# Sixteen squared sums and 48 PSUM copies moved from VectorE to ScalarE in a list-scheduled eight-core attention and feed-forward kernel

## What is computed

```python
z      = gelu_tanh(ln(x))
zn     = z / max(norm(z), 1e-12)                # per token
sim    = zn @ zn.T                              # per batch, 4096 x 4096
seq    = max of sim over earlier tokens         # strictly causal
ema    = zn . ema_norm                          # used alone for token 0
gate   = 1 - a + a * exp(-tau * (w * seq + (1 - w) * ema))
x      = x + z * gate
y      = ln(x)
g      = softmax(y @ gate_w.T)                  # 8 experts
x      = x + y @ weight.T + (1/16) * sum_e g_e * (y @ U_e.T) @ V_e.T
```

## Time and profile before

| | us |
|---|---|
| median of 2 runs | 374.4 (374.09 to 374.71) |
| the profiled execution, its own time | 373.94 |
| span of the slowest core in it (core 0) | 372.3 |
| span of the shortest core in it (core 6) | 362.0 |
| mean granted TensorE clock, core 0 / core 6 | 0.953 / 0.976 |

### The profile page before, as it was taken

One profiled execution on the slowest core, in us unless ns is written; L12 is line 12 of the kernel. 1 busy time (PEld: TensorE's weight loads), 2 busy tenths in 40 slices (PEclk: granted clock), 3 DMA queues, 4 the chain that ended last, 5 costly groups with the idle time before them and its releaser, 6 DMA issues.

```text
span 372.3 us, 5496 instructions; the slowest of 8 cores (362.0 to 372.3 us)
## 1 busy us (share of the span) xinstructions
PE 237.4 (64%) x1730; PEld 133.4 (36%) x1762; DVE 234.0 (63%) x537; ACT 147.8 (40%) x252; POOL 60.4 (16%) x38
## 2 busy tenths in 40 slices
PE   0010000246757758969978888978997687799891
PEld 0010000144434424525534444434553344454450
DVE  0222267785749664947754855396986887889452
ACT  2100008778474571391561193023443344443410
POOL 0000000635071526206224206100000000000000
PEclk9999999995789989989999999989998999999997
DMA  7977520245133331323203031511340022203422
GB/s 201 300 194 206 141 102 0 61 164 169 59 114 113 116 113 20 110 98 114 113 2 113 1 114 37 191 49 65 114 114 0 37 79 114 104 30 152 169 110 118
DMA packets 11664, 39.30 MB, mean 106 GB/s; under 512 B 1259, under 2 KB 2283, under 8 KB 11636
## 3 DMA queue, kind: packets, MB, share of 16 engines
q1 hardware_dynamic: 6528, 25.17, 19.2%
q10 hardware_dynamic: 5108, 13.78, 12.1%
HBM read 30.55 MB, written 8.39 MB: 105 GB/s over the span
## 4 chain that ended last, share of the span: by engine, by line
PE 38%; DVE 17%; ACT 16%; DMA 13%; issue 12%; POOL 2%; DVEq 1%; ACTq 0%; POOLq 0%; SPq 0%
PE ps L515 16%; PE ps L695 7%; PE ps L692 6%; ACT xbuf L430 5%; DMA xbuf<-wt 4%; DMA xbuf<-x 3%; DVE st L419 3%; PE ps L463 3%; ACT h L430 3%; ACT L430 3%; PE ps L686 3%; DVE st L418 2%; DVE colbuf L536 2%; DMA xbuf<-gw 2%; PE ps L665 2%
## 5 line engine op out<-in xcount | busy, mean ns | idle before, releaser
L515 PE MATMUL ps<-kT 128*128 128x512 bf16 (+3 forms) x621 | 134.5, 366 | 14.5 <-ACT kT L473 5.5
L515 PEld LDWEIGHTS ps<-kT 128*128 128x128 bf16 x640 | 53.8, 102 | 58.8 <-issue 20.6
L463 PE MATMUL ps<-identb,ktok 128*128 128x128 bf16 x256 | 22.2, 237 | 77.7 <-POOL ktok L454 52.2
L536 DVE TENSOR_REDUCE colbuf<-ps 128x1 f32<-128x512 f32 (+3 forms) x80 | 47.5, 602 | 17.1 <-PE ps L522 10.1
L454 POOL TENSOR_TENSOR ktok<-h,inv 128x1024 bf16<-128x1024 f32 x16 | 30.3, 1892 | 137.3 <-ACT rtmp L553 79.3
L695 PE MATMUL ps<-wTb,kT 128*128 128x512 bf16 x124 | 47.7, 385 | 0.9 <-DVE tgb L718 0.5
L692 PE MATMUL ps<-wTb,kT 128*128 128x512 bf16 x123 | 47.2, 384 | 0.2
L463 PEld LDWEIGHTS ps<-identb,ktok 128*128 128x128 bf16 x256 | 17.4, 106 | 81.7 <-issue 80.5
L473 ACT CAST kT<-ps 128x512 bf16<-128x512 f32 x32 | 18.5, 579 | 70.3 <-PE ps L463 65.1
L469 DVE CAST kT<-ps 128x512 bf16<-128x512 f32 x32 | 21.9, 684 | 25.1 <-PE ps L463 25.0
L454 POOL TENSOR_TENSOR ktok<-xbuf,inv 128x1024 bf16<-128x1024 f32 x16 | 30.3, 1893 | 35.4 <-PE ps L463 35.4
(11 more groups left out here) (98 smaller groups left out, 301.1 us busy)
## 6 DMA issues: line engine op xcount, KB each, us to landing
xbuf<-x SPq DMA_DIRECT2D x16, 1024.0 KB, 5.1
xbuf<-x ACTq DMA_DIRECT2D x8, 1024.0 KB, 5.5
y<-h SPq DMA_DIRECT2D x8, 1024.0 KB, 4.3
xbuf<-wt ACTq DMA_DIRECT2D x8, 512.0 KB, 4.5
xbuf<-ut ACTq DMA_DIRECT2D x1, 512.0 KB
xbuf<-vp ACTq DMA_DIRECT2D x1, 512.0 KB
xbuf<-gw ACTq DMA_DIRECT2D x1, 32.0 KB
identb<-ident ACTq DMA_DIRECT2D x1, 32.0 KB, 7.4
```

Of the source, the lines that this page charges most:

```text
L463: fns.append(lambda e, c=c, ps=ps: e.matmul(ps[:, (c % 4) * 128:(c % 4) * 128 + 128], ktok[:, buf, c * 128:(c + 1) * 128], ident[:, :], st ...
L515: fns.append(lambda e, c=c, pt=pts[bi], off=off, W=W, iswin=iswin: e.matmul(pt[:, 0:W], kT[:, c, 128 * m:128 * m + 128], kT[:, c, off:off ...
L536: p.op("vector", lambda e, pt=pts[bi], W=W, ci=cb_idx: e.reduce_max(colbuf[:, cbuf, ci:ci + 1], pt[:, 0:W], axis=AX), reads=[ptoks[bi]], w ...
```

## The change

Three steps change their engine, everywhere that they occur. The squared sum of the odd tiles (16 of the 32) goes from VectorE to ScalarE, so all 32 are ScalarE's. The copy of the first four transposed chunks goes from VectorE to ScalarE in the key phase (32 times) and in the second half (16 times), so both copies of each tile are ScalarE's. The costs in the planner's list go with them (1230 to 1150, 660 to 580). Reads, writes, buffers and matmuls stay as they were.

```diff
--- before.py
+++ after.py
@@ -434,15 +434,9 @@
             cost=1150.0, act_set="gelu")
         scr = xbuf[:, ri, :] if mine else ztile[:, 0, :]
         stok = ("xbuf", ri) if mine else ("zt", 0)
-        if tid % 2 == 0:
-            p.op("scalar", lambda e: e.activation(
-                scr, gdst, AF.Square, accum_out=ss8[:, g2, i:i + 1]),
-                reads=[gtok], writes=[stok, ("ss", g2, i)], cost=1150.0)
-        else:
-            p.op("vector", lambda e: e.scalar_tensor_tensor(
-                scr, gdst, 1.0, gdst, ALU.bypass, ALU.mult,
-                accum_out=ss8[:, g2, i:i + 1]),
-                reads=[gtok], writes=[stok, ("ss", g2, i)], cost=1230.0)
+        p.op("scalar", lambda e: e.activation(
+            scr, gdst, AF.Square, accum_out=ss8[:, g2, i:i + 1]),
+            reads=[gtok], writes=[stok, ("ss", g2, i)], cost=1150.0)
 
     def emit_key_tile_c(gi, i, tid, ri):
         g2 = gi % 2
@@ -466,10 +460,10 @@
                 start=(c % 4 == 0), stop=(c % 4 == 3), skip_group_check=True))
         p.op("tensor", fns, reads=[("ktok", buf), ("ident",)], writes=[ta, tb],
              cost=900.0)
-        p.op("vector", lambda e: e.tensor_copy(
+        p.op("scalar", lambda e: e.copy(
             kT[:, 0:4, col:col + 128],
             pa[:, :].rearrange("p (c f) -> p c f", c=4)),
-            reads=[ta], writes=[("kT", tid, 0)], cost=660.0)
+            reads=[ta], writes=[("kT", tid, 0)], cost=580.0)
         p.op("scalar", lambda e: e.copy(
             kT[:, 4:8, col:col + 128],
             pb[:, :].rearrange("p (c f) -> p c f", c=4)),
@@ -669,9 +663,9 @@
         p.op("tensor", fns, reads=[("z2", buf), ("ident",)], writes=[ta, tb],
              cost=900.0)
         col = 128 * m
-        p.op("vector", lambda e: e.tensor_copy(
+        p.op("scalar", lambda e: e.copy(
             kT[:, 0:4, col:col + 128], pa[:, :].rearrange("p (c f) -> p c f", c=4)),
-            reads=[ta], writes=[("kT", m, 0)], cost=660.0)
+            reads=[ta], writes=[("kT", m, 0)], cost=580.0)
         p.op("scalar", lambda e: e.copy(
             kT[:, 4:8, col:col + 128], pb[:, :].rearrange("p (c f) -> p c f", c=4)),
             reads=[tb], writes=[("kT", m, 1)], cost=580.0)
```

## The result

The changed kernel takes 388.9 us (median of 11 runs) against 374.2 us (10 runs of the kernel before): a ratio of 1.038, with a 95% interval from 1.035 to 1.042. The medians lie 14.7 us apart. The forecast was 377.9 us; the sign was right, the size was a quarter of what came. 388.9 is at the very edge of the stated range.

The account below looks back on a forecast made before the run. No engine carries the chain alone; it changes engines at nearly every step, with TensorE busiest. From the profiled 373.94 us, + 5.5 + 0.5 - 2.0 gave 377.9 us, with 366 to 389 as the 8-in-10 range.

Parts of the forecast that it names:

- Stretch 1: Early key phase, 56.5 to 126.5 us: ScalarE's added work makes it 5.5 us longer, bounds 0 and 15.4.
- a delay of 8.8 us: First four key-phase groups: two serial squared sums each, 1.1 us apiece, delay the Ln, before VectorE's relief is taken off.
- Stretch 2: Later key phase, 126.5 to 254 us: squared sums hidden, copy delays nearly offset by gains; +0.5 us, bounds -10 and +13.
- Rival A: Slower, 386 us, chance 0.27: ScalarE's queue decides when TensorE goes on; four later groups add 6, second half gains nothing.
- Stretch 3: Second half, 254 to 367 us: VectorE's relief frees a PSUM bank earlier in five slots; 2 us gained, bounds 7.6 gain, 7.4 loss.
- That the second copy ends ahead of L718: Second-half slots: both ScalarE copies end at about 303.5, hidden; without that cover the second costs 0.46 us a slot.
- The Trainium skill's rule: All 48 copy pairs: using both engines to empty PSUM speaks against the change; 22 us if all were on the path.
- The clock: Whole kernel: TensorE's mean clock should stay near 0.95; a fall was a cost put at nothing.
- The planner: Whole kernel: the list scheduler may reorder steps as VectorE's costs fall; large unknown, either direction, no size given.
- The waits for the copy line: Sign of being right: TensorE's waits name the key-copy line L473 more often; no size given.
- eight gelu loads: Key phase: more than eight gelu table loads would show the forecast wrong, groups torn apart at 2.6 us a time.
- the fifth: Fifth gelu table load, marking the early key phase's end: expected at about 132 us, from 126.5; no later means wrong.

Follow-up runs that it names:

- the last four groups moved: Kernel before, its order kept, with squared sums and key copies of only the last four of eight key-phase groups run on ScalarE: 382.6 us, ratio 1.027.
- the run in the old order: All 64 moved steps run on ScalarE, but planned with the engines, costs and order of the kernel before: 384.9 us, ratio 1.031 against it.
- the new order with the old engines: Changed kernel's plan and order, but every step runs on the engine of the kernel before: ratio 1.064 against that kernel, resting on two of six runs.
- the short squared sums: Changed kernel in its own order, with odd tiles' squared sums over 64 of 1024 columns: 381.4 us, ratio 1.022 against the kernel before.

## Why the prediction was right in its sign and wrong in its size

- **That ScalarE in series costs, and where VectorE's relief helps.** Right: squared sums cost, key copies cost in the key phase (in the total, 1.002, this is hidden), second-half copies gain. The total sign followed.
- **Stretch 1, +5.5.** The sum there gives 75.6 - 69.9 = 5.7, and the middle of its bounds of 0 and 15.4 is 7.7, not 5.5; both slips are small. Mis-sized: 9.6 us on core 0 and 8.1 by the median. ScalarE's work there was right (61.8 against 63.4); the idle time wasn't. Ahead of the key copies it was idle for 13.9 us, where I kept 4 of the 10.7. I took these waits for slack that new work would fill. They are not: the copy waits for transposes (the 13.9 us), and the transposes wait for the previous pair of copies in the same queue (the 26.0 us of TensorE's waits for L467). The squared sums in series, by which I argued for a delay of 8.8 us there, aren't what costs: alone they change this stretch from 70.0 to 69.8 us, key copies alone make it 74.6 and both 77.4. So the copies start the loss and squared sums add to it only on top of them. That the added work lengthens the loop from both ends is how I read this; no run takes the loop apart.
- **Stretch 2, +0.5.** This is the step that failed: "The squared sums should be hidden behind L515". They aren't. From the fifth load to the first normalisation the changed kernel lost 7.3 us by the median (4.9 on core 0), 4.4 of them up to the eighth load; squared sums alone lose 8.0 there. TensorE stood still for GpSimd for up to 4.9 us where it had not before. I argued from TensorE's share of 84% and from the older slots that it would have to work on; but in the sixth period the inverse norms had come 0.3 us before TensorE needed them, and the way from the gelu load to the Ln load got 2.1 us longer. The moved sums account for 1.6 us of each such wait, and the rest is TensorE having no older slot left. Rival A had the place and nearly the price (386, of which 6 in the later groups), by the cause of copies behind squared sums. That is one of the two ways, and the only one of them seen there in the old order; the inverse norms are the other. In the second half A had it wrong: it gave nothing back in the forecast's reckoning, and the runs show a gain.
- **Stretch 3, -2.** In the changed kernel itself it came to -0.7 us by the median and -1.7 on core 0. That this is near -2 is partly luck, since two things of more weight cancel: alone and in the old order the moved copies give 5.2 us, and the new order takes most of it away. The mechanism was right and its size too small, since nearly every slot gets shorter and not only the five whose wait the profile had put down to L718. That the second copy ends ahead of L718 was wrong; it became the next limit. The Trainium skill's rule of the page "TensorEngine Tiling (Array Packing)" (PSUM bottleneck, both engines for emptying PSUM) would have had these 16 pairs at a loss; here the measurement decides, a gain of 5.2 us, in a stretch where VectorE was the fuller engine (85.6 us of 113.0 against ScalarE's 42.9).
- **The clock.** I put it at nothing, and as a mean it is (0.952). In single stretches it isn't: long waits are followed by stretches at the lower of the two levels, as in the rows at 186.82 and 177.26. With the last four groups moved, the core that sets the time had this on top (0.941).
- **The planner.** I named it as the large unknown, and it was worth less than the move itself: some 0.7% of 3.8%, by the run in the old order. What in the new order costs it isn't settled; the new order with the old engines, at 6.4%, shows only that an order and an assignment go together. It also isn't shown why the key copies alone, in the planner's order, have 114.3 us from the first normalisation to the end, 6.6 less than before.
- **What was to show it.** The waits for the copy line grew, eight gelu loads stayed eight, the fifth came at 137.9 (I expected 132). ScalarE's 78% in stretch 1 was below the 85% named, and VectorE's busy time was 189.8 us where I named 178.

## What to carry to other kernels

Busy shares, and even busy shares by stage, don't price a move between in-order engines. Ask of each moved step who waits for it and what stands ahead of it in the new queue: a short copy that TensorE waits for costs little as work and much behind two gelus and two squared sums. Look at stretches and at the typical core as well as at the total: here a ratio of 1.002 hid a loss of 5.9 us and a gain of 6.6. An idle time that is part of a loop (copy, transposes, copy) is not room for new work. Where a list scheduler makes the order, test a move with the order held fixed: it shows what the move is worth, and here the same 16 copies gave -0.2% in the planner's order and -1.4% in the old one.

## What the runs showed that I had not expected

With an idle time of 4.39 us TensorE's granted clock fell from 1.00 to 0.50, that is from 2.4 to 1.2 GHz, and stayed there for some 4.7 us of work; over the period this makes 0.91. After 2.30 us at the same place it did not fall. In between it is not settled by the length of the wait: with the short squared sums, the transposes after 3.28 us on core 0 took 0.61 us, and after 3.29 us at the same place on core 2 they took 1.01. Cores of one execution differ by this: in the kernel before, the time from the fifth to the eighth table load is 84.2 us on three cores and 88.4 to 88.6 on five, in an identical program. In the fifth and sixth periods the three have granted clocks of 0.97 and 1.00, the five 0.94 and 0.93.
